# A decoder layer on one core: where the first two key tiles are weighed, and the order of a limit pass and a residual addition on VectorE

## What is computed

```python
x = _layernorm(x + attn(x, wq, wk, wv, wo))           # 16 heads of 32, 8 key/value heads, rope
x = _layernorm(x + xattn(x, ctx, Wq, Wkv, Wout))      # keys and values from ctx (4, 1601, 128)
x = _layernorm(x + ffn(x, nf4(w1), nf4(w2), nf4(w3))) # silu(x w1) * (x w2) w3, d_ff 1408
```

## Time and profile before

| | |
|---|---|
| median of 3 runs | 1163.75 us (1156.89 to 1165.9) |
| profiled execution | 1159.74 us, span of its instructions 1158.0 us |
| mean granted TensorE clock over the span | 0.973 of full speed |
| TensorE busy | 1036.7 us (90%) |
| VectorE busy | 761.2 us (66%) |
| ScalarE busy | 471.4 us (41%) |
| GpSimd busy | 464.9 us (40%) |
| attention | about 50 to 885 us: self to 504, cross from 504 |
| feed forward | about 885 us to the end |

### The profile page before, as it was taken

How to read it: one execution, slowest core, us unless ns; L and a number is a source line. 1 busy time by engine, 2 the same in 40 slices (tenths; PEclk the granted TensorE clock), 3 DMA queues, 4 the chain that set the end, 5 groups by cost and what they waited for, 6 DMA issues and landing times.

```text
span 1158.0 us, 17458 instructions
## 1 busy us (share of the span) xinstructions
PE 1036.7 (90%) x6248; PEld 668.0 (58%) x6248; DVE 761.2 (66%) x1566; ACT 471.4 (41%) x578; POOL 464.9 (40%) x492
## 2 busy tenths in 40 slices
PE   6789889988998889998889889889988999999995
PEld 5545445544554454456456555555645888888884
DVE  6786766647665669657865887777684636364545
ACT  3333343645355545555554566455443111212110
POOL 4437974896379555232342334232357400000000
PEclk9789999999899999999999999999999999999998
DMA  5731465568463855545474666548436301101020
GB/s 203 218 92 31 115 169 169 145 167 216 127 161 86 232 158 162 138 101 126 132 184 122 157 171 162 130 99 211 118 83 204 118 12 39 71 1 73 1 73 37
DMA packets 84290, 145.14 MB, mean 125 GB/s; under 512 B 15416, under 2 KB 32160, under 8 KB 83948
## 3 DMA queue, kind: packets, MB, share of 16 engines
q1 hardware_dynamic: 73180, 111.90, 36.5%
q0 software_dynamic: 9712, 31.34, 9.5%
q10 hardware_dynamic: 1312, 0.79, 0.2%
HBM read 78.09 MB, written 23.73 MB: 88 GB/s over the span
## 4 chain that ended last, share of the span: by engine, by line
PE 44%; DVE 12%; POOL 5%; issue 5%; ACT 3%; DMA 1%; SPq 0%; DVEq 0%; ACTq 0%; POOLq 0%
PE att_scores L1239 7%; PE att_pv L1239 7%; PE att_scores_T L1269 7%; PE att_pv L1014 7%; PE att_scores_T L941 4%; PE att_scores_T L943 4%; PE att_scores_T L942 3%; PE att_scores L957 2%; DVE att_scores L1582 2%; PE att_scores_T L990 1%; DVE att_mx L1587 1%; POOL att_pv_raw L756 1%; DMA att_probs<-nf_x 1%; DVE att_nf_zone L1738 1%; POOL att_probs L796 1%
## 5 line engine op out<-in xcount | busy, mean ns | idle before, releaser
L1404 ACT ACTIVATE att_probs<-att_scores_T 128x1024 f32<-128x1024 f32 (+2 forms) x256 | 219.9, 886 | 153.8 <-PE att_scores_T L990 150.8
L1014 PE MATMUL att_pv<-att_probs,att_v 128*32 128x512 f32 (+3 forms) x1024 | 216.8, 546 | 12.0 <-POOL att_probs L796 9.9
L1587 DVE TENSOR_REDUCE att_mx<-att_scores 128x2 f32<-128x1024 f32 x124 | 151.5, 1222 | 105.4 <-PE att_scores L957 104.8
L1014 PE MATMUL att_pv<-att_probs,att_ones 128*32 128x512 f32 (+3 forms) x1024 | 216.8, 547 | 0.0
L957 PE MATMUL att_scores<-att_k_stack,att_q_stack 96*128 96x256 f32 (+1 forms) x504 | 167.3, 405 | 36.8 <-DVE att_mx L1587 22.4
L990 PE MATMUL att_scores_T<-att_q_stack,att_k_stack 97*128 97x512 f32 (+2 forms) x512 | 137.4, 380 | 23.8 <-ACT att_raw L1341 13.4
L1582 DVE CUSTOM_DVE_ANT_0 att_scores<-att_scores,att_cmask 128x128 f32<-128x128 f32 (+3 forms) x256 | 120.6, 509 | 52.5 <-PE att_scores L957 52.3
L957 PEld LDWEIGHTS att_scores<-att_k_stack,att_q_stack 96*128 96x128 f32 x504 | 87.8, 193 | 86.5 <-DVE att_mx L1587 30.5
L796 POOL TENSOR_SCALAR_AFFINE_SELECT att_probs<-att_probs 128x256 f32<-128x256 f32 x128 | 60.1, 469 | 176.3 <-ACT att_probs L1404 171.4
L990 PEld LDWEIGHTS att_scores_T<-att_q_stack,att_k_stack 97*128 97x128 f32 x512 | 86.8, 192 | 61.3 <-issue 22.7
L1014 PEld LDWEIGHTS att_pv<-att_probs,att_v 128*32 128x32 f32 x1024 | 51.4, 112 | 114.5 <-issue 82.3
(11 more groups left out here) (254 smaller groups left out, 2115.3 us busy)
## 6 DMA issues: line engine op xcount, KB each, us to landing
att_q_stack<-att_q_hi SPq DMA_DIRECT2D x128, 128.0 KB, 3.3
att_probs<-nf_x SPq DMA_DIRECT2D x28, 352.0 KB, 3.5
att_nf_home<-nf_reciprocals POOLq DMA_DIRECT2D x48, 176.0 KB, 5.0
att_q_stack<-att_q_lo SPq DMA_DIRECT2D x64, 128.0 KB, 3.6
att_k_stack<-att_k_hi SPq DMA_DIRECT2D x64, 128.0 KB, 3.6
att_nf_home<-nf_x SPq DMA_DIRECT2D x20, 352.0 KB, 3.8
w_nf<-att_nf_zone SPq DMA_DIRECT2D x192, 22.0 KB, 2.4
att_k_stack<-att_k_hi SPq DMA_DIRECT2D x64, 64.0 KB, 3.5
```

Source lines behind the costliest of these rows:

```text
L1014: last = T.matmul(pv[HD * j:HD * j + HD, sums, q0:S], lhs, pr[:, at:at + S - q0], start=(t == 0), stop=(t == TT - 1))
L1404: A.activation(probs_of(b, r)[:, 1024 * h:1024 * h + w], bank[:, 0:w], ACT.Exp, scale=SCALE).then_inc(st_free, 1)
L1587: V.tensor_reduce(mx[:, p % 2, :].rearrange("p (r t) -> p r t", r=2)[:, :, t], sco[:, :, :], AX.X, ALU.max).then_inc(sc_free, 1)
```

## The change

Two edits. On TensorE, in self attention batches, a pair with work for the next batch weighs only tile 0 in front of it, and tile 1 behind the last maxima group and in front of the rounding. In crossed batches both tiles are weighed there. Pairs without such work stay as they were. On VectorE, in pair 1, pass 3 of the round `end` stands in front of the addition of the second output half and no longer behind it. Nothing is added or left out: each instruction is still issued once.

```diff
@@ -1175,10 +1175,9 @@
                     scores(b, p, 3)
                     mid, end = rounds_of(b, p)
 
-                    ahead = bool(whats) or p == 1 and b > 0
+                    ahead = not crossed(b) and (bool(whats) or p == 1 and b > 0)
                     if ahead:
                         weigh(b, p, 0)
-                        weigh(b, p, 1)
                     if p == 1 and b > 0:
                         project_out(b - 1, 0)
                         maxima(*fore, 2)
@@ -1196,7 +1195,7 @@
                         maxima(*fore, 3)
                     if not ahead:
                         weigh(b, p, 0)
-                        weigh(b, p, 1)
+                    weigh(b, p, 1)
                     if end is not None:
                         rounding(end)
                     if (b, p) == (0, 2):
@@ -1784,9 +1783,8 @@
                         if mid is not None:
                             scale_rounded(mid)
                         moments(b - 1, 0)
-                        exceeds(end, (1, 2))
+                        exceeds(end, (1, 2, 3))
                         add_residual(b - 1, 1)
-                        exceeds(end, (3,))
                         maxima(*fore, 3)
                         if end is not None:
                             scale_rounded(end)
```

## The result

The changed kernel takes 1148.75 us (median of 5 runs, 1140.64 to 1149.77) against 1160.89 us for the kernel before (5 runs, 1156.89 to 1165.9): a ratio of 0.988, with a 95% interval of 0.9851 to 0.9909. A second measurement of the same two kernels gave 0.9908 (0.9891 to 0.9925). The gain is 11 to 12 us, about 1%. The forecast was 1154.0 and 0.8%, with "within 1%" called the likeliest outcome. The profiled execution took 1148.54 us, 11.2 less than that of before.

What follows compares the result with a forecast made beforehand. TensorE, busy 90% of the span, and its waits bound the kernel. From 1159.74 us, -5.6 - 2.8 - 5.4 - 1.6 + 6.1 = -9.3 gives 1150.4; the 4.0 median offset makes 1154.4, range 1142 to 1168.

Steps and rivals of the forecast that it cites:

- Part 1: Limit pass in front of the addition, pair 1 of batches 1 to 3: 5.6 us gained, plus 2.8 of clock.
- Part 2: Self attention, tile 1 weighed behind the projections: front costs nothing, rounding and scaling waits shrink, 5.4 us gained.
- Part 3: Cross attention, both tiles behind, 20 steps: -1.6 us without the clock, +6.1 for falls.
- The three kinds: Cross attention steps: pair 3 gains, eight steps where VectorE sets the maxima lose 7.1 us, the others gain little or nothing.
- the clock's term: Granted clock: 2.8 us gained in batch 2, 3.6 new falls at 1.7 us in cross attention cost 6.1.
- The offset to the median: Whole kernel: median of the runs lies 4.0 us above the profiled run, so 1150.4 becomes 1154.4.
- (a): Rival: clock holds in cross attention and the gaps merely stand there; -15.4 us, 1148; chance 0.28.
- (b): Rival: VectorE sets every cross attention step, slower by 16 us, 1180, or half of it, 1172; chance 0.11.
- (c): Rival: no change, filled at one end and opened at the other, clock fall moves elsewhere; -3 to +3, 1164; chance 0.16.

Runs made afterwards that it cites:

- E1: Kernel before with only the limit pass moved in front of the addition; ratio 0.9943 (0.992 to 0.9965).
- E4: Changed kernel with cross attention as before, so both self attention edits together; ratio to before 0.9902 (0.9869 to 0.9936).
- E3: Kernel before with only the cross attention edit, both tiles weighed behind; ratio 0.9984 (0.9959 to 1.0008).
- E7: Changed kernel with part of the transposes of x issued three times over in pair 2 of batches 4 to 7; 1148.49 us, ratio to before 0.9882.
- E2: Kernel before with only tile 1 moved behind in self attention; ratio 0.9947 (0.9926 to 0.9968).
- again: The changed kernel, unaltered, measured and profiled a second time (the second execution); 1150.03 us, ratio to before 0.9908.
- E6: Changed kernel with tile 0 weighed ahead in cross attention, but none ahead in pairs 3 and 5; 1140.46 us, ratio to before 0.9817.
- E8: Changed kernel with tile 0 ahead in cross attention, but none in pair 3 and in pair 5 of batch 4; 1139.55 us, ratio to before 0.9816.
- E5: Changed kernel with tile 0 weighed ahead in cross attention too, in all pairs with such work; 1143.58 us, ratio to before 0.9845.

## Why the prediction was right or wrong

**Part 1, right in place and size.** Batch 2 was to gain 2.0 in pair 1 and gained 1.98; batch 3 was to gain 2.9 and gained 3.46 (2.95 in the second execution). In batch 1, pairs 0 and 1 together took 34.08 us before and 32.99 and 31.91 in the two executions (forecast 0.75 less; in the first, the output product waited 1.2 us for GpSimd). The rounding's wait for this pass came down to 3.3 us, not under 2: the forecast took all 8.4 us for pair 1's, but only 2.32 and 2.67 of them are, which went whole, and 2.85 stand in pair 0. Pass 3 was short at its new place in both (0.58 and 0.59 us), with GpSimd idle as the forecast said; the rule of the Trainium skill quoted in the prediction (GPSIMD Engine Reference, Specifications) agrees. But 2.55 us wasn't the price of a long pass, as the prediction took it: the last section shows that the pass ends 0.4 us after GpSimd's instruction, whatever that makes of its length. The pass moved in cross attention was costed at nothing; pair 2 of batches 4 and 6 became 0.40 shorter in both E1 and E4 (10.06 to 9.66), a gain that the forecast missed. By the runs of E1 the part is worth 5.1 us of the rest, where 5.6 was forecast.

**Part 2, right in mechanism, with one term wrong.** The wait for the scaling in pairs 2 to 4 went, 14.93 to 14.56 and 14.92 to 14.55 us: 0.37 where 0.36 was forecast. The two pairs 6 were to give 1.5 and lost 0.3 to 0.6 each instead. Between steps without a fall, that of batch 1 went from 18.5 (E1, E3) to 18.9 and 19.0 (E4, E7), that of batch 2 from 18.59 to 18.84. Parts 1 and 2 together, 11.0 without the clock, came to 7.8 and 9.2 against before and to 5.9 and 7.3 against E3's self attention, with half of the falls taken off, and to 9.0 by the runs of E4: too large by 2 to 5. Batches 1 to 3 became 7.0 and 7.7 us shorter, where 10 to 14 was to be seen.

**Part 3, nearly all of its steps right.** The three kinds behaved as told. Pair 3: -2.80, -1.51, -3.12 (forecast -2.6, -1.3, -2.9), and what is over -1.5 of it was clock, since E1 and E2 have the same unchanged step at 14.6 in one execution and 16.2 in another. Pair 4: +0.64, +0.63, +0.64; pair 2: +0.74 where no fall lies in it; pair 5 of batches 5 and 6 +0.29 and +0.82 (forecast +0.6 to +1.0). Pair 5 of batch 4: -0.89 (forecast -1.0). Pair 6 was -0.4 in batches 5 and 6 and +1.24 in batch 4, where ScalarE's 0.9 stayed and the weighings came behind it; this one the forecast had at -0.3. The new waits at the front are 20 with 12.7 us, 0.6 each, at the low end of the 0.5 to 1.0 forecast. The sum without the clock was -1.6. E3 measured -1.9 by its ratio (interval -4.8 to +0.9) and -0.2 in the rest, and the changed kernel has 2 us more of the rest than E4: nothing, or a small loss.

**The step that failed is the clock's term.** The forecast took the clock to cost 3.3 us in the whole (-2.8 in batch 2, +6.1 in cross attention); measured, it gave 3 to 5 us back: the changed kernel's runs lost 31.6 and 29.1 us by it, those of before 34.7 to 36.0. "I take 3.6 falls: +6.1" made waits of 1 to 2 us cause falls. The time at the lower clock in cross attention was 20.5, 10.2, 13.7 and 23.9 us in the four executions with two tiles ahead (before, E1, E2, E4), and 17.1, 13.7, 10.2 and 20.5 in the four with none (changed, again, E3, E7). Nothing was added: the means are 17.1 with two ahead and 15.4 with none. E3's runs, where only those waits are new, lost 33.8 us by the clock against 34.7. In the same way the 2.8 us from the fall in batch 2 was no certain gain: the first execution still has one at 308.7 us, the second none, and there the step became 1.7 us shorter (18.01 to 16.32). The falls are a cost of every version, and part of them lie elsewhere from one execution to the next. A term for the clock should have stood in the range only. The other terms of the sum, -12.6 together, were too large in their turn: 7 to 8 us of waits went. So two errors of opposite sign, about 5 us in the waits and 6 to 8 in the clock, left a sum of -9.3 beside the measured 11: that this came out near is luck.

**The offset to the median** was the second term mis-sized. The profile of before lay 4.0 under the median of its three runs, and this was added to the changed kernel's forecast. Its own profile lay 0.2 under its median, and the medians of before in later measurements were 1160.9, 1159.5, 1163.3 and 1161.1. Of the 5.7 us between the sum's 1154.4 and 1148.75, this is 3.8, and the sum's 9.3 instead of 11.2 is 1.9. Both pulled the same way, from just over 1% to just under it.

**The rivals.** (a), the clock holds in cross attention, is what the falls and the runs of E3 show. Its time of 1148 was met, but not by its own sum: it saved 15.4 and the medians 11 to 12, and the offset of 4.0 made up the rest. (b), VectorE setting every step, is refuted by pair 3 and by E3. (c), no change, fails on E1 and E2; its mechanism, that what is filled at one end is opened at the other, is what cross attention did.

**Open:** which executions get which falls, and why the changed kernel's runs lost 4 to 7 us less by the clock than those of before, when its single profiles show about as much time at the lower clock.

## What to carry to other kernels

Work that one engine can do early or late covers a wait at the one place and opens one at the other. Ask for each step which of the two waits is longer than the piece, and try to split the work between both sides. Here one weighing on each side gave 4 to 7 us more than all in front (E4) or all behind (the changed kernel), and with both behind in pairs 3 and 5 where GpSimd is late (E6, E8) 7 to 11. Where several waits end almost together (a rounding for a pass, a score group for the scaling), try the edits together too: in these steps each alone showed less than its share.

## What the runs showed of the hardware

The same pass of VectorE, 128x1408 bf16, took 0.58 us with GpSimd idle, 1.32 and 1.87 (E2) beside GpSimd's product L689, and 2.55 beside a DMA issue and then the product L712. The lengths hide a simple rule of this case. In before the product is

```profile
305.69 2.35 POOL L689 TENSOR_TENSOR att_x_lo<-att_x_in,att_x_hi 128x1024 fp32r<-128x1024 f32 x1 [13.90 <-ACT att_x_hi L1357]
```

and ends at 308.04, the pass at 308.42. In E2 the two ends are 304.64 and 305.02, in the earlier trace rows 429.75 and 430.14. Every pass (L1738) of before that took over 0.7 us, 17 in all, ended 0.38 or 0.39 us after a GpSimd instruction that lay over it. So a pass that meets such an instruction costs the rest of that instruction and 0.4 us more, and a length from another place is no price for it. The moved pass isn't safe everywhere: in batch 1 of E5 it met L712 and took 1.68. The Trainium skill (GPSIMD Engine Reference, section Specifications) says that the two share their SBUF interfaces; these ends agree.

Between 100 and 885 us the granted clock fell in 5 to 9 places in each execution, for 3.4 to 13.7 us, and three of the eight places differed between two executions of one program: the second of the changed kernel had none at 308.7, 592.0 and 636.4 and had others at 120.6, 366.3 and 537.0. The wait of 1.11 us at one place of pair 2 was followed by a fall in one and by none in the other. The Trainium skill (TensorE: Matmul & The Clock Gate, Part 1) has the clock follow how busy TensorE has been. No run here contradicts that, and none shows which of these waits brings a fall.
